# Dense attention: how early the row maxima of the next head are taken, when the edge work is interleaved, and when GpSimd begins to split the edges

## The reference, cut to what matters

```python
# first layer (_L0_conv_ref): 4 heads of 32 channels
h = _group_norm(x, gn_gamma, gn_beta)
qkv = einsum('oc,bchw->bohw', qkv_w, h) + qkv_b
attn = softmax(einsum('bhdn,bhdm->bhnm', q, k) * scale, axis=-1)
out = einsum('bhnm,bhdm->bhdn', attn, v)
return x + einsum('oc,bchw->bohw', proj_w, out) + proj_b
...
# fourth attention (_L3_attn_ref, global_mha): 8 heads of 16 channels, beside a local attention and two MLPs
attn = softmax(einsum('bqhd,bkhd->bhqk', q, k) / sqrt(hd), axis=-1)
o = einsum('bhqk,bkhd->bqhd', attn, v)
```

## Time and profile before

| | |
|---|---|
| median of 3 executions | 2445.96 us (2445.37 to 2446.14) |
| the profiled execution | 2440.69 us, of which its instructions span 2439.0 us |
| busy over the span | PE 1869.7 us (77%), DVE 1559.3 us (64%), ACT 1039.3 us (43%), POOL 719.0 us (29%) |
| mean granted clock of TensorE | 0.841 of full speed |
| maxima of the first layer (L797), 256 | 161.1 us busy |
| maxima of the fourth layer (L2460), 512 | 334.9 us busy |

### The profile page before, as it was taken

One profiled execution on the slowest core, in us unless ns is written; L12 is line 12 of the kernel. 1 busy time (PEld: TensorE's weight loads), 2 busy tenths in 40 slices (PEclk: granted clock), 3 DMA queues, 4 the chain that ended last, 5 costly groups with the idle time before them and its releaser, 6 DMA issues. The chain is left out here.

```text
span 2439.0 us, 26403 instructions
## 1 busy us (share of the span) xinstructions
PE 1869.7 (77%) x8810; PEld 846.6 (35%) x8810; DVE 1559.3 (64%) x3609; ACT 1039.3 (43%) x1724; POOL 719.0 (29%) x703
## 2 busy tenths in 40 slices
PE   2966995796688476689957888878878888978494
PEld 1213321321232134456631222222322324864264
DVE  4687777768777685556716575665566554635647
ACT  1333141233314116545533667657656653214255
POOL 3302600630270041024441322332322321127740
PEclk7878897888789787889966999989988986759797
DMA  7002100300120000021001111101011000014100
GB/s 197 1 21 59 44 2 25 77 17 20 50 52 3 25 1 1 1 102 21 14 30 51 42 31 40 41 17 40 29 29 38 3 5 15 1 54 62 10 7 35
DMA packets 55445, 80.16 MB, mean 33 GB/s; under 512 B 17249, under 2 KB 28504, under 8 KB 55073
## 3 DMA queue, kind: packets, MB, share of 16 engines
q1 hardware_dynamic: 44806, 69.14, 9.6%
q10 hardware_dynamic: 6426, 7.99, 1.5%
q0 software_dynamic: 4096, 1.58, 1.4%
HBM read 50.13 MB, written 24.68 MB: 31 GB/s over the span
## 5 line engine op out<-in xcount | busy, mean ns | idle before, releaser
L2460 DVE TENSOR_REDUCE f_half_max<-f_ring 128x1 f32<-128x512 f32 x512 | 334.9, 684 | 272.9 <-PE f_ring L2126 270.8
L2343 ACT ACTIVATE f_probs<-f_ST 128x512 f32<-128x512 f32 x512 | 293.0, 597 | 210.6 <-PE f_ST L2153 206.5
L2126 PE MATMUL f_ring<-f_stacks 96*128 96x512 bf16 x512 | 212.0, 415 | 54.5 <-DVE f_half_max L2460 28.1
L797 DVE TENSOR_REDUCE att_half_max<-att_ring 128x1 f32<-128x512 f32 x256 | 161.1, 683 | 88.1 <-PE att_ring L684 87.0
L2153 PE MATMUL f_ST<-f_stacks 99*128 99x512 bf16 x512 | 204.7, 405 | 10.3 <-ACT f_probs L2343 10.3
L780 ACT ACTIVATE att_probs<-att_ST 128x1024 f32<-128x1024 f32 x128 | 129.3, 1023 | 157.5 <-PE att_ST L709 157.3
L2170 PE MATMUL f_O<-f_probs,f_v_ext 128*32 128x512 f32 x1024 | 154.1, 677 | 0.1
L3182 POOL DMA_INDIRECT ti_row<-features,slot_from x128 | 127.9, 999 | 56.8 <-issue 56.8
L2126 PEld LDWEIGHTS f_ring<-f_stacks 96*128 96x128 bf16 x512 | 50.4, 99 | 258.8 <-DVE f_half_max L2460 162.6
L727 PE MATMUL att_O<-att_probs,v_ext 128*64 128x512 f32 x512 | 134.5, 652 | 6.4 <-DVE att_den L816 6.4
L709 PE MATMUL att_ST<-stacks 96*128 96x512 bf16 (+1 forms) x512 | 137.7, 397 | 0.0
(11 more groups left out here) (588 smaller groups left out, 3507.5 us busy)
## 6 DMA issues: line engine op xcount, KB each, us to landing
f_stacks<-f_parts SPq DMA_DIRECT2D x192, 64.0 KB, 2.2
parts_dram<-l_parts SPq DMA_DIRECT2D x8, 768.0 KB, 3.6
stacks<-parts_dram SPq DMA_DIRECT2D x24, 256.0 KB, 9.7
stacks<-parts_dram ACTq DMA_DIRECT2D x24, 256.0 KB, 10.8
f_parts<-f_parts SPq DMA_DIRECT2D x8, 768.0 KB, 3.5
es_raw<-L_ffn_edge_index SPq DMA_DIRECT2D x8, 512.0 KB, 4.6
bm_mix<-mix SPq DMA_DIRECT2D x8, 512.0 KB, 9.0
xn_cm<-x SPq DMA_DIRECT2D x4, 512.0 KB, 4.2
```

Of the source, the lines that this page charges most:

```text
L797: nc.vector.tensor_reduce(half_max[:, h % 2, t, n:n + 1], ring[:, i % RING], AX.X, ALU.max, negate=True).then_inc(reduced, 1)
L2126: nc.tensor.matmul(ring[:, i % RING], f.stacks[0:STACK, 0, at, t * P:(t + 1) * P], f.stacks[0:STACK, 1, at, n * BANK:(n + 1) * BANK], star ...
L2343: nc.scalar.activation(f.probs[:, s % PROBS, n * BANK:(n + 1) * BANK], ST[:, i % HALVES], ACT.Exp).then_inc(probs_ready, 1)
L2460: nc.vector.tensor_reduce(f.half_max[:, h % 2, t, n:n + 1], ring[:, i % RING], AX.X, ALU.max, negate=True).then_inc(reduced, 1)
```

## The change

Three things. (1) In both schedules, the look-ahead at step s is no longer 2 row tiles above one a step from the start but min(s + 2, 2(s - 1)), at least 0. Row tiles taken in steps 0, 1, 2, 3, 4 were 3, 1, 1, 1, 1 and are 0, 2, 2, 2, 1; from step 4 on the schedules are the same. (2) VectorE makes two edge calls a step from step 18 on (before: from step 22), and the loop that does what is left of the edge work stands behind the normalisation. (3) GpSimd waits for the first head's parts (`parts_ready` at 1) before it splits.

```diff
+    def ahead(s):
+        return max(min(s + AHEAD, 2 * (s - 1)), 0)
+
     schedule("first", tiles(0, in_group))
     for h in range(share):
         schedule_rows("first", h)
     for s in range(len(steps)):
-        r = s + in_group + AHEAD
-        schedule(s, tiles(in_group if s == 0 else r, r + 1))
+        schedule(s, tiles(in_group + ahead(s), in_group + ahead(s + 1)))
...
                 if beside is not None and s >= EDGES_FROM:
-                    for _ in range(1 if s < in_group + AHEAD + EDGES_FROM - 2 else 2):
+                    for _ in range(1 if s < EDGES_FROM + 4 else 2):
                         next(edge_steps, None)
-            if beside is not None:
-                for _ in edge_steps:
-                    pass
             if share == 1:
                 carry_off(groups - 1)
                 dve.wait_ge(off_by_dve, NC2 * groups)
...
                 nc.vector.tensor_tensor(chunk(o_cm, n), chunk(o_cm, n), chunk(den, n), ALU.mult).then_inc(normed, 1)
+            if beside is not None:
+                for _ in edge_steps:
+                    pass
             for n in range(NC2):
                 dve.wait_ge(projected, n + 1)
...
             def _(pool):
+                pool.wait_ge(parts_ready, 1)
                 beside.split(pool, edges_loaded, edges_linked, edges_coded)
...
# fourth_layer_stream
+    def ahead(s):
+        return max(min(s + f.AHEAD, 2 * (s - 1)), 0)
+
     for s in range(len(steps)):
-        r = s + IN_GROUP + f.AHEAD
-        schedule(s, IN_GROUP if s == 0 else r, r + 1)
+        schedule(s, IN_GROUP + ahead(s), IN_GROUP + ahead(s + 1))
```

## The result

The changed kernel took 2474.47 us (median of 4, 2468.47 to 2478.81) against 2445.66 us (2444.64 to 2446.14) for the kernel before, measured beside it: a ratio of 1.0118, interval 1.0101 to 1.0135. It is slower, as forecast, but by 28.8 us where 6.7 were forecast: 2452.7 us was expected, with a range up to 2460. The profiled execution took 2473.73 us, with a span of 2472.0 us at a mean granted clock of 0.837.

The account below looks back on a forecast made before the run. No engine was full over the span: TensorE bound the middle, VectorE was late from step 18. Terms 4 x 1.26 + 4 x 1.1 - 2.29 - 0.5 = +6.7 us gave 2447.4 profiled, 2452.7 as median; range 2442 to 2460.

Parts of the forecast that it names:

- the look-ahead's term: First layer, start of each dense attention: first mix +1.1 us later an image, bounds -1.0 and +3.1.
- the clock rising when it did: Start of each dense attention: TensorE's clock assumed to rise as in the kernel before, giving +1.1 us an image.
- at 1.2 GHz throughout: Upper bound at the start: 28 matmuls of 0.43 us from 71.45 end at 83.5, so +3.1 us.
- The split under the second head's parts: GpSimd's later split overlaps the second head's parts: a stall covered, taken as 0, bounds 0 and +1.0 us an image.
- the rival built on it: Three two-input operations of the second head's parts each wait for GpSimd: 24 us in all, 2476.7 us; chance 0.05.
- The fourth layer: First maxima to first mix, once: new look-ahead gains -0.5 us, bounds -1.9 and +1.1.
- The tail: End of each dense attention: head 2's carry-off 4.18 us later, last carry-off +1.26 us an image, bounds -2.97 and +2.99.
- the leftover loop: Edge work moved behind the normalisation: the 25 calls are used up earlier in both kernels, so it changes nothing.
- The chain of the first parts: Small VectorE operations before the first head's parts, no longer stretched by GpSimd's split: -2.29 us over four images.
- the marker: Sign in the new profile: TensorE's wait for att_den still before the last head's mix, 18 edge calls ahead of that copy.
- The rival of the clock falling before the last head's mix: TensorE's longer stand there drops its clock: 6.9 us more over four images, 2459.6 us; chance 0.15.

Follow-up runs that it names:

- b1: The changed kernel with one idle matmul of 384 columns ahead of the fourth look-ahead tile of steps 1 to 3; ratio 1.0112 to the kernel before.
- b2: The changed kernel with a step's transposed scores put between its first two and last two look-ahead tiles; ratio 1.0104 to the kernel before.
- g1: b2 with GpSimd's split in two, five instructions after the first head's parts and three after the second's; ratio 1.0059 to the kernel before.
- d1: The changed kernel with GpSimd's split in two, five instructions after the first head's parts and three after the second's; ratio 1.0099 to the kernel before.
- e2: The kernel before with GpSimd's split in two and edge calls from step 11, one a step until step 25, then two; ratio 1.0005.
- a2: The kernel before with only two edge calls a step from step 18 on and the leftover loop moved; ratio 1.0052.
- g2: g1 with the edge calls paced as in the kernel before (two a step from step 22); ratio 0.9994 to the kernel before.
- f1: The changed kernel with the fourth layer's look-ahead as in the kernel before; ratio 1.0086 to the kernel before.
- c1: The kernel before with edge calls from step 8 (before: 14), one a step until step 25, then two; ratio 1.0024.
- h1: The kernel before with GpSimd's split in two and edge calls from step 8, one a step until step 25, then two; ratio 1.001.

## Why the prediction was wrong

*The step that failed* is in the look-ahead's term: "the clock rising when it did". The working had TensorE at 2.4 GHz from about 8 us after the parts; it stayed at 1.2 GHz until 15.6 to 17.4. The first mix is then later by 3.1 to 3.6 us an image instead of 1.1, and itself takes 3.53 us instead of 1.94. The upper bound, "at 1.2 GHz throughout", was in the text at +3.1, and what happened lies at it or a little beyond (+3.4 in image 1); the value was taken well below it, though the same paragraph counts on the ring's three banks, which is what makes TensorE stand. b1, b2 and g1 show it from the other side: without the stand-stills the clock rises at 5.3 to 8.6 and the mix comes at 10.9 to 12.2, in all their images but one. The bound also ended at the first mix, while the clock stayed low into the mix; a bound on a clock has to run until the clock is back.

*The split under the second head's parts* was costed at 0, with 1.0 an image as the upper end; d1 shows 1.0. The error is in how a row was read. The text puts all stretched operations down to two inputs, but those of images 3 and 4 in the earlier trace rows are conversions, with one. And in the earlier trace rows an operation of 0.87 us ends long before the GpSimd instruction of 2.79 us above it, which was held against the rule of the Trainium skill ("SBUF — State Buffer", section "Who interferes with whom") that the later of the two blocks fully. That GpSimd instruction has one input. In all 18 profiles, 39 operations of the parts began under a GpSimd instruction with two inputs, and all 39 (27 with two inputs, 12 conversions) stood until it ended, within 0.07 us. So the rule holds there, and the rival built on it was underrated in kind; its price of 24 us was still too high, since not every operation meets such an instruction, and tiles cover some of it. Under a GpSimd instruction with one input, 45 of 51 two-input operations took their usual 0.17 us, so there the measurement goes against the rule's wording. Conversions to bf16 stood until the end in 19 of 43 cases. There the moment of the start decides: the seven operations of either kind that began in the first 0.2 us of a GpSimd instruction with one input (2.8 us) stood until some 1.06 us after its start; two-input operations that began later, from 0.96 us on, all took their usual time; conversions that began later took theirs with 1.07 us or more left, and stood until the end with 0.65 to 1.00 us left.

*The fourth layer* was costed at -0.5. The first mix did move by -1.2, within its bounds, but the stream is longer by 7.2 us. It does not arise in one place: against the kernel before the changed one is 0.9 us ahead at the 130th exponential, 2.8 behind at the 260th, 4.4 at the 455th and 7.2 at the last. It is at 1.2 GHz for 115 of the first 700 us, the kernel before for 105. Why the clock falls there is not settled: a different start shifts everything behind it, and e2, without the look-ahead, also ended at 750.9.

*What was right.* The tail: head 2's carry-off 4.2 us later was forecast, 4.2 to 4.4 measured, the last carry-off moving over to TensorE, +1.35 an image against +1.26, and the leftover loop empty. a2 shows it without the other edits, g1 with TensorE at full clock, and g2 undoes it. The chain of the first parts: -2.27 against -2.29. Only the marker was wrong: the wait was to stay with att_den, and it went to the last head's parts and to the exponential. The rival of the clock falling before the last head's mix does not occur in the changed kernel's profile. That is luck: f1, whose first layer is the same code, has it in images 1 and 2, and a2, b1, b2, d1 and g1 have it in some or all; there it costs 1.6 an image, where 1.73 was forecast. In the changed kernel the clock falls earlier in the tail, 72 to 74 us after the parts and behind the new wait for the last head's parts, and is back before the mix begins.

*What lies outside the edits* is +4.3 between the images. Its code is the same. From one image's last carry-off to the next image's first maximum it takes 114.3 to 114.9 us before and 115.0 to 115.7 in the changed kernel; the others, c1 and h1 left aside, range from 113.9 to 116.6. So it may be scatter of single profiles, part of the 33.0 that the median's 28.8 does not have; that is not shown.

## What to carry to other kernels

Where a matrix engine has just been idle, cost the next steps at its low clock until a row shows that it has come back, also through the work behind them, and look at how many buffers the new order needs at once, since a wait for a bank in each step went with a low clock here. Whether the clock comes back early can differ from image to image with the same code, so reckon with both. When moving one engine's side work, list every small operation of the other engine that it will now run under, and not only the one that it is moved away from. An edit that only moves a bottleneck's own work earlier gained about 1 us an image here, and cost clock where it landed; before such an edit is given up, see in the trace whether its loss lies in the stretch that it touches, which in c1 and h1 it did not.

## What the runs showed of the hardware

Waits of TensorE of some 0.1 us a step, with 13.41 of 14.19 us busy, went with a clock that stayed at 1.2 GHz; filling them with a useless matmul brought the first mix 2 to 3 us forward. The same code at the same place rose at 5.6 and at 15.4 us after the parts in two images of one execution.

Falls have a sign, too: in the dense attentions of the kernel before and the changed one, each of the 8 and 11 falls between the first mix and the last head's came 1.6 to 3.8 us after TensorE had begun to stand for 1.57 to 2.06 us. A stand of 1.57 us passed without a fall in image 1 of the changed kernel, 44.7 us after the parts.

Under a GpSimd instruction with two inputs (2.35 us) every small VectorE operation stood until it ended and took up to 2.36 us instead of 0.17. Under one with a single input it depended on the kind of the operation and on when it began.
